# Four instead of two stationary-weight tiles in rotation in a ternary feed-forward stage

## The reference, cut to what matters

```python
def bitlinear(x, w):
    return jnp.einsum('bsh,oh->bso', act_quant(x), weight_quant(w))
def h_bitlinear(x, w):
    return jnp.einsum('bsh,oh->bso', act_quant(fwht(x)), weight_quant(w))
gate = bitlinear(x, w_gate)          # w_gate, w_up: 8192 x 2048
up = bitlinear(x, w_up)
intermediate = jax.nn.silu(gate) * up
return h_bitlinear(intermediate, w_down)   # w_down: 2048 x 8192
```

## Time and profile before

| | us |
|---|---|
| median of 2 runs | 9545.05 (9498.25 to 9591.85) |
| the profiled execution, own time | 9511.19 |
| its span (core 7, the slowest) | 9509.6 |
| spans of the eight cores | 9410.2 to 9509.6 |
| TensorE matmul busy | 4472.2 (47%) |
| TensorE weight load busy | 2644.2 |
| VectorE busy | 4000.0 (42%) |
| ScalarE busy | 212.5 (2%) |
| DMA, mean over the span | 121 GB/s |

### The profile page before, as it was taken

The page is one execution under the profiler, slowest core; times in us unless marked ns, Lnnn a source line. Parts: engine busy times, 40 slices in busy tenths (PEclk is TensorE's granted clock), DMA queues, the critical chain, the costliest instruction groups (busy, mean ns, idle before and its releaser), DMA issues. The chain is left out here.

```text
span 9509.6 us, 81513 instructions; the slowest of 8 cores (9410.2 to 9509.6 us)
## 1 busy us (share of the span) xinstructions
PE 4472.2 (47%) x31174; PEld 2644.2 (28%) x31174; DVE 4000.0 (42%) x3071; ACT 212.5 (2%) x271; POOL 0.2 (0%) x4
## 2 busy tenths in 40 slices
PE   7745547244734547245603334404465166236705
PEld 1112213243212213243201222302254045225504
DVE  0143342334343332433486555596514701740191
ACT  0000000000000000000000000000000000000000
POOL 0000000000000000000000000000000000000000
PEclk9877768555867768556856565656698599679958
DMA  7623342301433342301516777507753155135405
GB/s 240 196 78 97 120 150 71 124 28 31 147 107 119 99 148 68 122 28 51 165 47 154 183 183 181 149 0 219 216 182 109 32 183 190 39 102 181 160 0 160
DMA packets 992618, 1154.81 MB, mean 121 GB/s; under 512 B 110314, under 2 KB 798699, under 8 KB 966635
## 3 DMA queue, kind: packets, MB, share of 16 engines
q1 hardware_dynamic: 992236, 1149.60, 40.8%
HBM read 1006.83 MB, written 142.66 MB: 121 GB/s over the span
## 5 line engine op out<-in xcount | busy, mean ns | idle before, releaser
L619 PE MATMUL pbk<-BA 128*128 128x512 bf16 x4608 | 1195.0, 427 | 1142.0 <-DVE BA L567 1142.0
L1353 PE MATMUL pbk<-BA 128*128 128x256 bf16 x8192 | 1172.0, 305 | 1144.6 <-DVE BA L1312 789.4
L1353 PEld LDWEIGHTS pbk<-BA 128*128 128x128 bf16 x8192 | 852.4, 108 | 1465.5 <-issue 1291.3
L1549 PE MATMUL pbk<-BA 128*128 128x256 bf16 x4096 | 604.6, 313 | 966.1 <-DMA BA<-tD 563.9
L619 PEld LDWEIGHTS pbk<-BA 128*128 128x128 bf16 x4608 | 488.9, 107 | 1824.0 <-issue 1408.3
L1549 PEld LDWEIGHTS pbk<-BA 128*128 128x128 bf16 x4096 | 438.1, 111 | 1134.2 <-issue 1037.9
L448 DVE TENSOR_REDUCE redp<-AR 128x1 f32<-128x2048 f32 x192 | 438.8, 2286 | 367.0 <-DMA AR<-wuT 129.4
L702 PE MATMUL pbk<-BA 32*32 32x32 bf16 x6144 | 344.9, 223 | 431.1 <-PEq L663 431.1
L702 PEld LDWEIGHTS pbk<-BA 32*32 32x32 bf16 x6144 | 344.2, 145 | 433.3 <-issue 433.3
L1318 DVE TENSOR_TENSOR qt<-pbk,AR 128x512 f32<-128x512 f32 x128 | 88.5, 692 | 892.8 <-PE pbk L1353 887.8
L278 PE MATMUL pbk<-AR,cfm 128*1 128x512 f32 x768 | 341.7, 605 | 53.4 <-DMA AR<-wmod 49.6
(11 more groups left out here) (179 smaller groups left out, 3484.2 us busy)
## 6 DMA issues: line engine op xcount, KB each, us to landing
AR<-wgT SPq DMA_DIRECT2D x128, 1024.0 KB, 10.2
AR<-wuT SPq DMA_DIRECT2D x128, 1024.0 KB, 10.6
AR<-wdT SPq DMA_DIRECT2D x128, 1024.0 KB, 7.1
AR<-wmod SPq DMA_DIRECT2D x24, 4096.0 KB, 16.0
BA<-tG SPq DMA_DIRECT2D x192, 512.0 KB, 3.3
BA<-tU SPq DMA_DIRECT2D x192, 512.0 KB, 3.4
BA<-tD SPq DMA_DIRECT2D x192, 512.0 KB, 3.8
AR<-wqT SPq DMA_DIRECT2D x32, 1024.0 KB, 6.3
```

Of the source, the lines that this page charges most:

```text
L619: mm = t.matmul(bank[:, :], wof[:, ci * 128:(ci + 1) * 128], mv[:, ci * 512:(ci + 1) * 512], start=first, stop=(wof is wsL and ci == 15))
L1353: mm = t.matmul(bank[:, slot * QT:slot * QT + QT], bav(tern_of(j), 2048)[:, ci * 128:(ci + 1) * 128], h2q_all[:, ci * 1024 + q4 * QT:ci * ...
L1549: mm = t.matmul(pbk[fo % 2][:, 0:QT], bav(tern_of(j), 2048)[:, ci * 128:(ci + 1) * 128], zqv(k), start=(k == 0), stop=(k == 63))
```

## The change

It gives quarters 1 to 3 four places for the ternary tiles in place of two. `tbuf4(j)` is j mod 4: places 0 and 1 are those in `BA`, places 2 and 3 are in a new buffer `TB2` (128 x 4096 bf16). The load of tile j now waits for the end of group j-4. TensorE reads its weight blocks from the same place. Quarter 0 keeps two places. The returned `nbuf` tells the next quarter how many places the last down stage used, for the waits of its first four loads.

To make room in SBUF, `qt1` and `qt2` shrink from 1024 to 512 columns, `lrow` moves into `AR4`, and the work tile of `emit_h2q` (before quarter 0) moves from `qt1` to `AR4`. Shapes and types of the instructions stay.

```diff
-    lrow = sball("lrow", [1, 256])
-    qt1 = sball("qt1", [128, 1024])
-    qt2 = sball("qt2", [128, 1024])
+    TB2 = sball("TB2", [128, 4096], BF16)
+    qt1 = sball("qt1", [128, 512])
+    qt2 = sball("qt2", [128, 512])
+    lrow = AR4[0:1, 0:256]
...
-                    t1 = qt1[:, 0:1024]
+                    t1 = f32v(AR4, 8192, 1024)
...
+        def tbuf4(j):
+            r = j % 4
+            if r < 2:
+                return bav(16384 + r * 2048, 2048)
+            return TB2[:, (r - 2) * 2048:(r - 2) * 2048 + 2048]
...
-                        if j >= 2:
-                            waits = [(sPE.h, pe_b + j - 1)]
+                        if j >= 4:
+                            waits = [(sPE.h, pe_b + j - 3)]
                         elif prev is not None:
-                            waits = [(sPE.h, prev['down_pe_end'] - 1 + j)]
-                            if prev['down_spl'][j] is not None:
+                            nb_p = prev['nbuf']
+                            waits = []
+                            if j < nb_p:
+                                waits.append((sPE.h, prev['down_pe_end'] - nb_p + j + 1))
+                            if j < 2 and prev['down_spl'][j] is not None:
                                 waits.append(prev['down_spl'][j])
                         else:
                             waits = []
                         ld_toks.append(PL.load(
-                            q, bav(tern_of(j), 2048),
+                            q, tbuf4(j),
                             scr[:, oc * 2048:(oc + 1) * 2048], waits=waits))
...
+                    tsrc = bav(tern_of(j), 2048) if q4 == 0 else tbuf4(j)
                     for ci in range(16):
                         mm = t.matmul(bank[:, slot * QT:slot * QT + QT],
-                                      bav(tern_of(j), 2048)[:, ci * 128:(ci + 1) * 128],
+                                      tsrc[:, ci * 128:(ci + 1) * 128],
...
-                            waits = ([(sPE.h, pe_b + j - 1)] if j >= 2
-                                     else [(sPE.h, gup_pe_end - 1 + j)])
+                            waits = ([(sPE.h, pe_b + j - 3)] if j >= 4
+                                     else [(sPE.h, gup_pe_end - 4 + j + 1)])
                             ld_toks.append(PL.load(
-                                q, bav(tern_of(j), 2048),
+                                q, tbuf4(j),
                                 tD[:, j * 2048:(j + 1) * 2048], waits=waits))
```

More of the change, by code:

```diff
@@ L1555, in emit_ffn_quarter @@
                 'down_pe_end': pe_b + 64, 'y15': y_toks[15],
-                'down_spl': (spl_toks.get(62), spl_toks.get(63))}
+                'down_spl': (spl_toks.get(62), spl_toks.get(63)),
+                'nbuf': 2 if q4 == 0 else 4}
     emit_h2q()
```

## The result

The changed kernel is faster: 8992 us against 9505 us in the median (11 and 10 runs), 512 us less. The ratio and its interval, 0.9434 (95%: 0.9396 to 0.9472), are of the executions alone in which no die ran behind the other at a lower clock; by it the change is worth 5.7%, or about 540 us. The forecast was 8930 us in a range of 8830 to 9110. The profiled execution of the changed kernel took 8947.42 us.

A forecast was written before the change was run, and what follows sets the result against it. The prediction took load latency with two places to bound gate and up and down. 710 + 384 + 8 = 1102 us against 1700, 598 less, gave 8913, or 8947 with the median's offset; forecast 8930 us, range 8830 to 9110.

The forecast's parts named there:

- The bound: Gate and up and down, quarters 1 to 3: load latency with two places bounds them, 2.85 and 3.1 us a group.
- Gate and up, 710 us: Gate and up, quarters 1 to 3: 384 groups at 1.85 us, TensorE's 1.75 plus 0.10 allowed, against 1079.4 us before.
- Down, 384 us: Down, quarters 1 to 3: 192 groups at 2.0 us, a little over the DMA rate's 1.95, against 620.9 us before.
- the step on SP's order: Down: SP waits at the store for the evacuation, so a block's first tile load leaves about 0.4 us late.
- a DMA rate of 303 GB/s: Down: 2.36 MB per four groups at this rate, from 185 / 0.61, takes 7.8 us, 1.95 a group.
- Sum and offset: Whole kernel: 1102 us against 1700, 598 less, gives 8913; with the median's 34 us offset 8947; the middle, 8930, was forecast.
- its 8 for their heads: Six stretches: the first two groups of each run partly at the lower clock, 1.5 us each, about 8 us in sum.
- The DMA ceiling of 250 GB/s: Rival in both stages: DMA delivers less than demanded, 2.10 and 2.36 us a group, 9078 or 9112 us; chance 0.17.
- The store's round trip: Rival in down: evacuation waits for the previous block's store, 2.45 us a group, 8999 or 9033 us; chance 0.09.
- The change did what it says: Answers a rival in both stages: landings grow in step with loads in flight, so no change, 9511 us; chance 0.03.
- The clock: Rival in both stages: TensorE loses 2.4 GHz when all cores multiply densely; partly 9086 us, chance 0.05; wholly 9769, 0.02.
- the output projection's 1.00: Evidence against the clock rivals: in the output projection TensorE was busy 50 of 50 us at granted clock 1.00.

The follow-up runs named there:

- the later store: Changed kernel with down's store of block fo-2 and residual load behind the block's first tile load, result buffer in two halves: 9051 and 9064 us.
- the run with everything: Changed kernel plus eight places, down's store and residual load behind four tile loads, next stages' first tiles loaded early, four staging tiles in quarter 0: 8680 us median.
- early tiles: Changed kernel plus the later store, with the first four tiles of each next stage loaded at the end of the stage before: ratio 0.9376 to the kernel before.

## Why the prediction was right

**The bound.** That both stages were a loop of one load's latency over two places, and not short of TensorE or DMA, is shown. In gate and up the loop (landing + 0.5 + 1.9) / places gives 2.85, 2.33 and 1.83 us for two, three and four places with the landings of each, and 2.81, 2.31 and 1.89 were measured; with half tiles and two places it gives 2.6 against 2.53. In down, with the landings of all cores, it gives 3.1, 2.43 and 1.94 against 3.10, 2.49 and 2.07, so with four places some 0.13 us there is not in it.

**Gate and up, 710 us.** Measured on core 7: 721. The number was right and its make-up was not. I let the loop fall to 1.43 us with an unchanged landing, and added 0.10 to TensorE's 1.75 for late landings and the clock. The landing grew to a median of 4.9 us, above the 4.7 that I said costs nothing (by the loop it is 4 x 1.75 - 2.4 = 4.6), so with four places the loop itself stands at 1.83. The runs with eight places and without loads show that none of the 0.13 is TensorE's.

**Down, 384 us.** Measured: 391. Here the step on SP's order failed: I had the first tile load of a block leave 0.4 us late behind the evacuation's wait, and it leaves 0.26 us after its place is free in the mean, 0.09 in the median. What costs the time is the landing of the tiles, 5.3 to 5.6 us for all four of a block, where I had counted on 3.8; that the two small transfers cause the part above gate and up's 4.9 is likely, as the later store moved the gap with them, but not shown by itself. The other step, a DMA rate of 303 GB/s from share and rate, was too low as a ceiling: the changed kernel moves 287, below it, and the run with everything 328. So 384 was near 391 for reasons that were in part wrong.

**Sum and offset.** On core 7 the whole became 598 us shorter, as forecast, but to the microsecond that is luck: the six stretches came out at 1112 us where the sum had 1102 with its 8 for their heads, and 10 us were won outside them. And core 7 was no typical core in down: 3.23 us a group where the eight cores had 3.10. In its quarters 2 and 3 some 12% of the matmuls took 0.42 us, the lower of the two clock levels (granted clock 0.93 over these stretches). Over the eight cores the stretches became 554 us shorter and the spans 535; the ratio gives 538, the medians 512. The term that was too large is therefore the step from one core to the kernel: I took the slowest core's sum for the time, and after the change another core is the slowest. The rest, 18 us in the mean, lies mostly ahead of the touched stages: VectorE's loop in `emit_h2q`, ahead of quarter 0, begins 14 us later on average in this execution, behind code that is unchanged. That loop with its moved work tile lasts 69.4 us in both. Whether the 14 us come from the execution or from the kernel is not told by one trace of each.

**The rivals.** The DMA ceiling of 250 GB/s did not come: core 7 moved 280 in gate and up with four places, and core 2 moved 300 with eight, while the other cores ran the same stage. That fits the share of about 358 GB/s per core in the Trainium skill, "HBM Reference", Specifications (TRN2), the section that the prediction meant with Access; the highest that a run here shows is 328. The store's round trip did not come: in the changed kernel every evacuation starts 0.2 to 0.6 us after its block's last group, as before, so none waits for a store, though the stores land after 4.4 us. The change did what it says. The clock, which I had given 0.05, is absent from the profiled execution but came in others (last section).

## What to carry to other kernels

When an engine idles before every tile, and neither it nor the DMA engines are full, write the loop down: landing plus queue time plus the work on one tile, over the number of places. Place n + 1 pays until the loop falls below the engine's own pace, but the landing has to be taken at the new rate, since it grows with the bytes under way. And where two things may bound the prefetch, places and an issuing queue that stands at another wait, try them together too before dropping either: in down neither alone gave more than 0.03 us a group, and the run with both, and one more change of order, gave 0.25.

## What the runs showed of the hardware

**Landings grow with the bytes in flight well below a full DMA.** A 512 KB tile landed after 3.3 us at 182 GB/s, 4.6 at 227 and 4.9 at 280, at shares of 0.54, 0.74 and 0.86. A 256 KB tile took 2.8 us with two places, at 105 GB/s, and 3.0 with four, at 150 GB/s and a share of 0.52. In down with eight places, at 328 GB/s and a share of 1.01, a 512 KB tile took 10.6 us. Whether the growth comes from the core's own DMA engines or from the other cores at the same memory was not told apart.

**TensorE's clock between its two levels.** In some executions some cores show a granted clock of 0.81 to 0.84 over a whole stretch, with or without loads. The matmul line then has this form (line 1366, eight places, gate and up in quarter 1, core 0 and then core 2; ns min/median/max):

```profile
L1366 PE MATMUL pbk<-BA x512: 272/306/417, 6855.3 to 7109.3; 128*128 128x256 bf16 x171
```

```profile
L1366 PE MATMUL pbk<-BA x512: 272/273/422, 6950.5 to 7165.6; 128*128 128x256 bf16 x171
```

That is neither the level of 2.4 GHz nor that of 1.2. The Trainium skill, "TensorE: Matmul & The Clock Gate", Seeing it yourself, describes a third state of 13/16 for a die once three of its cores multiply densely. The rows fit the level, and the prediction was wrong to let the output projection's 1.00 speak against it as a whole. The condition does not fit as simply: in the run without loads cores 6 and 7 fell in two of three quarters while cores 4 and 5 of the same die, just as busy, stayed at 0.99, and in the profiled execution of the changed kernel no core fell in these stages. It came in pairs of cores: 0 and 1 with half tiles and two places, 6 and 7 without loads and with the later store, 0, 1, 6 and 7 with eight places, 2 to 5 with early tiles. What decides it is open.

It also comes where TensorE has idle time, and it costs there too. With half tiles and two places, cores 0 and 1 fell in quarter 2; the window is of core 0, the line of core 1:

```profile
7720.00:8040.00 320.00, 267.96 (x1942) 201.02 (x1940) 41.56 (x61) 20.18 (x31) 0.00 (x0) 0.82 0.34 100
```

```profile
L1353 PE MATMUL pbk<-BA x2048: 269/306/421, 7726.1 to 8067.4; 128*128 128x256 bf16 x187
```

What it costs grows with the pace of the stage. Gate and up of these two cores took 338 and 342 us where their other quarters took 322 and 324, 5% more; where the clock was under 0.84 over a whole stretch, one of some 241 us with four places became 265 to 271, 10% to 12% more, and one of 226 without loads or with eight places became 262 to 268, 16% to 19% more.
